# Cross attention on one core: denominators from columns of ones beside the values, a fifth score bank, and an exponential in two parts

## The reference

```python
x = (hidden - mu) * rsqrt(var + eps) * gamma + beta        # hidden: 32 x 56 x 512
Q = split_heads(x @ Wq.T)                                  # 32 heads of 16
K = V = split_heads(ctx)                                   # ctx: 32 x 1500 x 512
scores = einsum('bhsd,bhtd->bhst', Q, K) * 16 ** -0.5      # masked where the mask is false
attn = einsum('bhsd', softmax(scores) @ V)
out = hidden + attn @ Wout.T
```

## Time and profile before

| | |
|---|---|
| median of 3 runs | 1465.87 us (1465.43 to 1465.91) |
| span of the profiled execution | 1461.6 us |
| TensorE busy, matmuls | 1404.7 us (96%), 30000 records |
| VectorE busy | 1079.4 us (74%) |
| ScalarE busy | 750.7 us (51%) |
| GpSimd busy | 1243.8 us (85%) |
| granted TensorE clock, mean | 0.993 |

### The profile page before, as it was taken

How to read it: one execution, slowest core, us unless ns; L and a number is a source line. 1 busy time by engine, 2 the same in 40 slices (tenths; PEclk the granted TensorE clock), 3 DMA queues, 4 the chain that set the end, 5 groups by cost and what they waited for, 6 DMA issues and landing times.

```text
span 1461.6 us, 66063 instructions
## 1 busy us (share of the span) xinstructions
PE 1404.7 (96%) x30000; PEld 992.2 (68%) x30000; DVE 1079.4 (74%) x3356; ACT 750.7 (51%) x623; POOL 1243.8 (85%) x434
## 2 busy tenths in 40 slices
PE   6999999999999999999999999999999999999986
PEld 4346667776777777766776776777777777766765
DVE  6657777777777777777787777777777777777730
ACT  2125555555555555555555555555555555555553
POOL 1009999999999999989999898999999999999996
PEclk8989999999999999999999999999999999999999
DMA  9303444444444344444544434354443444444320
GB/s 297 81 33 148 165 162 160 157 158 168 162 168 172 145 172 157 160 170 147 180 150 166 164 146 175 145 187 160 156 166 142 182 161 161 170 165 156 143 79 21
DMA packets 39161, 224.90 MB, mean 154 GB/s; under 512 B 4546, under 2 KB 4578, under 8 KB 26882
## 3 DMA queue, kind: packets, MB, share of 16 engines
q1 hardware_dynamic: 38882, 220.68, 41.5%
HBM read 216.90 MB, written 3.77 MB: 151 GB/s over the span
## 4 chain that ended last, share of the span: by engine, by line
PE 81%; DVE 10%; ACT 6%; issue 1%; DMA 1%; POOL 1%; ACTq 0%; SPq 0%; DVEq 0%; POOLq 0%
PE ps L237 23%; PE ps L292 19%; PE ps L277 17%; DVE masked L338 9%; PE ps L306 6%; PE ps L269 6%; ACT probs L373 6%; PE ps L254 4%; PE ps L670 4%; PE ps L245 1%; POOL sums L425 1%; DMA v<-in_wq_t 0%; DVE probs L578 0%; DVE den_inv L362 0%; PE ps L661 0%
## 5 line engine op out<-in xcount | busy, mean ns | idle before, releaser
L338 DVE CUSTOM_DVE_ANT_0 masked<-ps,mask_tile 112x500 bf16<-112x500 f32 x1536 | 980.0, 674 | 304.9 <-PE ps L237 286.0
L373 ACT ACTIVATE probs<-ps,mask_bias 125x1792 f32<-125x1792 f32 x384 | 673.9, 1755 | 616.6 <-PE ps L277 609.5
L425 POOL TENSOR_TENSOR sums<-sums,probs 125x1792 f32<-125x1792 f32 x191 | 763.1, 3995 | 14.6 <-ACT probs L373 5.7
L425 POOL TENSOR_TENSOR sums<-probs 125x1792 f32<-125x1792 f32 x96 | 383.7, 3997 | 179.5 <-ACT probs L373 177.9
L237 PE MATMUL ps<-kT,qdb 32*112 32x500 bf16 x1536 | 485.5, 413 | 19.6 <-DVE tile_max L338 15.7
L277 PEld LDWEIGHTS ps<-qd,kT 32*125 32x125 f32 x12288 | 423.7, 184 | 1.9 <-issue 0.9
L277 PE MATMUL ps<-qd,kT 32*125 32x112 f32 x12288 | 421.4, 268 | 0.8 <-issue 0.6
L292 PE MATMUL ps<-probs,v 125*32 125x112 f32 x12288 | 373.1, 261 | 2.1 <-issue 1.3
L292 PEld LDWEIGHTS ps<-probs,v 125*32 125x32 f32 x12288 | 298.8, 110 | 70.0 <-issue 46.2
L237 PEld LDWEIGHTS ps<-kT,qdb 32*112 32x112 bf16 x1536 | 161.3, 123 | 217.2 <-DVE tile_max L338 151.2
L269 PE MATMUL ps<-max_rows,ones_row 4*125 4x448 bf16 x1536 | 179.6, 392 | 14.3 <-ACT probs L373 11.1
(11 more groups left out here) (49 smaller groups left out, 256.2 us busy)
## 6 DMA issues: line engine op xcount, KB each, us to landing
kT<-in_kt SPq DMA_DIRECT2D x96, 1000.0 KB, 5.1
v<-in_ctx SPq DMA_DIRECT2D x96, 1000.0 KB
mask_tile<-mask_add SPq DMA_DIRECT2D x32, 328.1 KB, 13.7
x_res<-in_x SPq DMA_DIRECT2D x16, 224.0 KB, 14.3
out<-result SPq DMA_DIRECT2D x16, 224.0 KB, 13.9
probs<-in_x SPq DMA_DIRECT2D x14, 224.0 KB, 9.2
v<-in_wq_t SPq DMA_DIRECT2D x1, 1024.0 KB, 6.1
woutT<-in_wout_t SPq DMA_DIRECT2D x1, 1024.0 KB, 20.6
```

The costliest lines, as they stand in the source:

```text
L338: nc.vector.tensor_tensor_reduce(out=masked[0:PAIR_Q, t % 2, :], in0=bank[0:PAIR_Q, 0:KEYS], in1=mask_tile[0:PAIR_Q, b % 2, KEYS * c:KEYS ...
L373: nc.scalar.activation(probs[0:LANES, k % PROBS], ps[0:LANES, 0:TILES_R, 0:BANK_Q], ACT.Exp, bias=mask_bias[0:LANES, n:n + 1], scale=SCALE ...
L425: nc.gpsimd.tensor_tensor(total, before, probs[0:LANES, slot % PROBS], ALU.add).then_inc(summed, 1)
```

## The change

- **Values.** A chunk of values is loaded into a staging buffer (`v_stage`, two of them). GpSimd copies it (`spread_values`) into `v`, where each pair of heads now has 48 columns: 16 of one head, 16 of ones, 16 of the other. The ones are set once.
- **times_values.** 32 matmuls instead of 16, each with 56 columns of `probs` (one head's queries) and 32 weight columns: this head's 16 values and the 16 ones. The product has the head's output in one half of the rows and its denominator in the other.
- **Sums.** `add_slot`, `add_denominators` and `last_denominators` are gone. ScalarE copies the whole accumulator once a batch (`take_acc`), GpSimd picks the halves (`fold_heads`: two multiplications of 448 columns, two additions of 224), VectorE swaps halves of the denominators within 32 partitions (`swap_denominators`, behind t1 of slot 3), and inverts them as before.
- **Score banks.** Bank 5 is free of denominators. Row tile 3 of the scores alternates between banks 3 and 5. The exponential is two instructions: banks 0 to 2 (125x1344), then the fourth (125x448). The scores of the next slot wait for the first part alone, and for the second part of the slot before the last.
- **Rows.** The turned maxima go through the ring of banks 6 and 7 as a unit of their own, in slot 10 between t2 and t3; VectorE copies them out and GpSimd spreads them.

```diff
-            wait_over(pe, exped, SLOTS * b + k)
+            n = SLOTS * b + k
+            wait_over(pe, exped_held, n)
+            wait_over(pe, exped, n - 1)
...
         def times_values(pe, b, k):
-                pe.wait_ge(v_landed[c], 16 * (b + 1))
+                pe.wait_ge(v_ready, CHUNKS * b + c + 1)
+            pe.wait_ge(exped, SLOTS * b + k + 1)
             if k == 0:
-                wait_over(pe, heads_taken, b)
-            for g in range(BLOCKS):
+                wait_over(pe, acc_taken, b)
+            for i in range(HEAD_GROUPS):
+                g, e = i // 2, i % 2
                 for r in range(TILES_R):
-                    mm = nc.tensor.matmul(acc[ROW * r:ROW * (r + 1), g, :], v[0:LANES, c, k % CHUNK, col:col + ROW],
-                                          probs[0:LANES, k % PROBS, r, PAIR_Q * g:PAIR_Q * (g + 1)],
+                    mm = nc.tensor.matmul(acc[ROW * r:ROW * (r + 1), i, :],
+                                          v[0:LANES, c, k % CHUNK, TILES_R * g + r, HEAD_DIM * e:HEAD_DIM * e + ROW],
+                                          probs[0:LANES, k % PROBS, r, QUERIES * i:QUERIES * (i + 1)],
...
+            nc.scalar.activation(probs[0:LANES, k % PROBS, 0:HELD_ROWS], ps[0:LANES, 0:HELD_ROWS, 0:BANK_Q], ACT.Exp,
+                                 bias=bias, scale=SCALE).then_inc(exped_held, 1)
+            nc.scalar.activation(probs[0:LANES, k % PROBS, HELD_ROWS], ps[0:LANES, score_bank(n, HELD_ROWS), 0:BANK_Q],
+                                 ACT.Exp, bias=bias, scale=SCALE).then_inc(exped, 1)
...
+        def spread_values(pool, b, c):
+            n = CHUNKS * b + c
+            pool.wait_ge(v_landed[n % STAGES], 16 * (n // STAGES + 1))
+            wait_over(pool, pv_done, CHUNK * (n - CHUNKS + 1))
+            halves = v[0:LANES, c].rearrange("p k i (h d) -> p (k i) h d", d=HEAD_DIM)[:, :, 0:3:2, :]
+            staged = v_stage[0:LANES, n % STAGES].rearrange("p k (i h d) -> p (k i) h d", h=2, d=HEAD_DIM)
+            nc.gpsimd.tensor_copy(halves, staged).then_inc(v_ready, 1)
...
+        def fold_heads(pool, b):
+            pool.wait_ge(acc_taken, b + 1)
+            pick_half(picked_den, 1).then_inc(den_picked, 1)
+            pick_half(picked, 0).then_inc(head_picked, 1)
...
+            nc.gpsimd.tensor_tensor(den_across[:], picked_den[:, :, 0], picked_den[:, :, 1], ALU.add).then_inc(den_added, 1)
...
-                for a in range(ADDS):
-                    if (b, a) != (end, ADDS - 1):
-                        add_slot(pool, b, a)
...
-                    if k >= 6 and (k - 6) % GROUP < 2:
-                        add_denominators(pe, b, (k - 6) // GROUP, (k - 6) % GROUP)
-                    elif k in (2, 3) and b > 0:
-                        add_denominators(pe, b - 1, SUMS - 1, k - 2)
-                    if k == ROWS_SLOT and b < end:
-                        turn_rows(pe, b + 1)
+                    for unit in slot_rows(b, k):
+                        turn_rows(pe, unit)
```

More of the change, by code:

```diff
@@ L28 @@
 PROBS = 4
-GROUP = 4
-SUMS = SLOTS // GROUP
-ADDS = SUMS * (GROUP - 1)
+HEAD_GROUPS = 2 * BLOCKS
+PAIR_COLS = 3 * HEAD_DIM
+STAGES = 2
+RING_BANKS = [6, 7]
+HELD_ROWS = TILES_R - 1
+LAST_ROW_BANKS = [3, 5]
+ACC_BANK = 4
+SWAP_AT = (3, 1)
 INVERT_AT = [(3, 3), (4, 0), (4, 2), (4, 3)]
 ROWS_SLOT = 10
+HALVES_SWAPPED = [(lane + HEAD_DIM) % ROW for lane in range(ROW)]
 OUT_PARTS = 4
@@ L59, in slot_others, with slot_rows, slot_units @@
             if slot == k and after % 2 == b % 2 and b >= after]
+def slot_rows(b, k):
+    return [("rows", b + 1)] if k == ROWS_SLOT and b + 1 < BATCH else []
+def slot_units(b, k):
+    tiles = slot_tiles(b, k)
+    return tiles[0:3] + slot_rows(b, k) + tiles[3:4] + slot_others(b, k)
 FIRST_TILES = [("tile", 0, t) for t in range(MAX_TILES)] + [("tile", 1, t) for t in range(AHEAD)]
-RING = FIRST_TILES[:]
-RING += [unit for b in range(BATCH) for k in range(SLOTS) for unit in slot_tiles(b, k) + slot_others(b, k)]
+RING = FIRST_TILES + [("rows", 0)]
+RING += [unit for b in range(BATCH) for k in range(SLOTS) for unit in slot_units(b, k)]
 LAST_OUTS = [("out", d, part) for d in range(BATCH // 2 - 2, BATCH // 2) for part in range(OUT_PARTS)]
@@ L312, in last_denominators @@
-        def last_denominators(pe):
-            pe.wait_ge(summed, ADDS * BATCH - 1)
-            for source in (sums[0:LANES, (SUMS * BATCH - 1) % 2], probs[0:LANES, (SLOTS - 1) % PROBS]):
-                for e in range(2):
-                    for r in range(TILES_R):
-                        own_q = source[:, r, :].rearrange("p (g e q) -> p g e q", g=BLOCKS, e=2)[:, :, e, :]
-                        mm = nc.tensor.matmul(den[ROW * r:ROW * (r + 1), :, :], ones[0:LANES, e, :], own_q,
-                                              start=False, stop=True, skip_group_check=True,
-                                              tile_position=(0, ROW * r))
-            mm.then_inc(den_done, 1)
@@ L338, in take_tile @@
             nc.vector.tensor_tensor_reduce(
-                out=masked[0:PAIR_Q, t % 2, :], in0=bank[0:PAIR_Q, 0:KEYS],
+                out=sums, in0=bank[0:PAIR_Q, 0:KEYS],
                 in1=mask_tile[0:PAIR_Q, b % 2, KEYS * c:KEYS * (c + 1)], scale=1.0, scalar=LOWEST,
@@ L595, in _ @@
             take_max(dve, 0)
-            for unit in FIRST_TILES[MAX_TILES:]:
+            for unit in FIRST_TILES[MAX_TILES:] + [("rows", 0)]:
                 take_unit(dve, unit)
```

227 lines of the change are left out of this document (114 added, 113 removed).

## The result

The changed kernel takes 1586.73 us in the median of four runs (1581.49 to 1588.83), against 1465.65 (1464.49 to 1465.91) for the kernel before on the same chip: a ratio of 1.0825, 95% interval 1.0805 to 1.0845. It is slower by 121 us, where 1413.0 (1396 to 1445) was forecast.

The account below looks back on a forecast made before the run. It took a loop over VectorE's two tiles and TensorE's values to bound ordinary slots. Terms -47.0 - 1.2 - 5.8 + 1.5 = -52.5 us gave 1409.1 profiled, 1413.4 in all; 1398 to 1430 at chance 0.72, stated range 1396 to 1445.

Parts of the forecast that it names:

- What bounds the kernel: Ordinary slots: a loop over VectorE's two tiles and TensorE's values, 3.44 us with L306, 3.05 without.
- the exponential's loop: Scores, exponential, next scores: 3.23 us a slot, bare in the last batch, elsewhere only delaying scores inside a slot.
- the split: Exponential in two parts: its loop falls from 3.23 to 2.86 us, no gain of its own in ordinary slots.
- Denominators: Taking L306 off TensorE: five slots of a batch gain 0.39 us each, 1.95 us a batch.
- copies: GpSimd's three copies of 2048 elements a batch: 4.6 us each taken, range 2.3 to 4.57, hidden.
- end: After the last slot: denominators through ScalarE's copy, picks, an addition and a shuffle before the inversions, about 1.5 us more.
- the cover over GpSimd: GpSimd's chain to slot 3's denominators: 13.6 us with 16.0 available, hidden until a copy takes 5.8 us.
- the turned maxima stand in the ring: Slot 10: the turned maxima wait until VectorE has taken t1, no gain there and a loss of 0.08 us.
- Values: the step that failed: Values in 64 records for 32, priced by columns: 0.02 us more a slot, 0.25 a batch.
- the floor for narrow matmuls: Case in the list of chances called only the floor: 1425 us, chance 0.08.
- the rival of values by the record: Values limited by issue, not columns: 1.54 us a slot, 1701 us; chance 0.10, wholly or in part and slower.
- Signs given: Profile after: values 0.92 us, t3 to t3 3.07, last batch 2.86 a slot; wrong if the batch stays above 41.

Follow-up runs that it names:

- the 112-column kernel: Changed kernel with 16 values matmuls of 112 columns instead of 32 of 56, one head's output of each pair left out: 1408.42 us, ratio 0.9609.
- the new denominators with one exponential: Changed kernel with 16 values matmuls of 112 columns and the exponential again one instruction over four banks, bank 5 unused: 1446.9 us, ratio 0.9874.
- a quarter: Changed kernel whose loads bring only a quarter of keys (from the third batch) and values (from the second): 1486.49 us, ratio 1.0125.
- next to nothing loaded: Changed kernel whose loads bring only 32 columns of each chunk of keys (from the third batch) and values (from the second): 1440.34 us, ratio 0.9844.
- with 56 columns: Kernel before with its values in 32 matmuls of 56 columns instead of 16 of 112, same result: 1596.45 us, ratio 1.0907.
- half and half: Changed kernel with 24 values matmuls a slot, in each row tile four of 56 columns and two of 112: 1455.02 us.

## Why the prediction was wrong, step by step

*What bounds the kernel.* Right for the changed kernel, half right for the one before. t3, VectorE's two tiles, t2, values is a loop of 3.44 with L306 and 3.05 without; the 112-column kernel runs at 3.06. Its middle batches take 40.57 us in the mean; the forecast of 42.11 - 1.62, without the 0.25 for narrow matmuls, was 40.24. But I wrote of the kernel before that the exponential's loop only delays scores inside a slot. There L269 waits for it 217 times, and slots 1, 2, 5 and 6 take 3.24 from scores to scores, with L306 or without:

```profile
PEld ps L269 <- ACT probs L373: 64.7, 217, 1.3
```

Both loops hold that kernel. So the new denominators with one exponential give little, 18 us, and the split, which I priced at nothing of its own in ordinary slots, 38; their sum of 56 is near the forecast's 52.5 and the 8 that the narrow matmuls were to take.

*Denominators, split, copies, end.* Right, as terms. With 112 columns the whole comes to 1408.42 where the working gave 1405 once the extra matmuls' price was out. ScalarE's parts take 1381 and 626 ns (1.38 and 0.5 to 0.6 said), VectorE's copy and its shuffle 274 and 407 (some 0.2 and 0.3 said, from no row), and GpSimd's copies 1.89 us, less even than the lower end of 2.3; the other end of that range, 4.57, was the one I took, and it was hidden all the same.

```profile
L385 ACT ACTIVATE probs<-ps,mask_bias 125x1344 f32<-125x1344 f32 x384 | 530.3, 1381 | 711.9 <-PE ps L303 711.9
...
L387 ACT ACTIVATE probs<-ps,mask_bias 125x448 f32<-125x448 f32 x384 | 240.4, 626 | 0.0
...
L429 POOL COPY v<-v_stage 125x2048 f32<-125x2048 f32 x96 | 181.5, 1891 | 75.5 <-DMA v_stage<-in_ctx 75.4
```

The last slots, without tiles, run at 1543.34, 1546.18, 1549.02: 2.84 each, for the forecast of 2.86 and the 3.23 of the earlier trace rows.

```profile
1543.34 0.41 PE L295 MATMUL ps<-max_rows,ones_row 4*125 4x448 bf16 x4 [0.65 <-ACT probs L385]
...
1546.18 0.41 PE L295 MATMUL ps<-max_rows,ones_row 4*125 4x448 bf16 x4 [0.65 <-ACT probs L385]
...
1549.02 0.41 PE L295 MATMUL ps<-max_rows,ones_row 4*125 4x448 bf16 x4 [0.65 <-ACT probs L385]
```

VectorE waits for the swapped denominators (`den` on `den_across`) only in two batches of 32, so the cover over GpSimd held. In slot 10 L269 now waits for VectorE 0.83 each time (24.9 us in 30), because the turned maxima stand in the ring. It costs what the earlier trace rows gave, 0.08: from t3 to t3 slot 10 takes 5.08 in the 112-column kernel, for 5.01 before.

*Values: the step that failed.* The working took 0.02 a slot for the narrow matmuls, 0.25 a batch; they cost 5.49 a batch (46.06 for 40.57). As the pace of the matmuls 0.02 is right. 64 records end after 0.99, groups of four start 0.049 apart, as worked out from columns. A price by the record, 1.54 for 64 records, is out with that. No run shows the floor for narrow matmuls that the recorded chances name (1425): the groups of 56 columns start 0.049 apart, half of the 0.096 between groups of 112 in the trace of before. What I did not price is the supply. I wrote "TensorE must now take 104 pairs of load and matmul in a slot for 72" in the rival of values by the record, but looked for a limit only in the values' own 0.77 us ("by the record, 1.54"), not in how long 256 instructions have to last. The row that would have told it was on the page of before and I left it out: 236 packets in 1461.6 us, one every 6.2 us, and 5.4 by the records of an ordinary slot. The forecast needed one every 3.8 us in ordinary slots and every 4.1 in the mean of a batch (40.49 us for 2554 instructions), beside 1 MB loads. This is a rival that should have had a good chance, with a price that no row could give.

*The rival's mechanism.* Its outcome (slower than before) came, with 0.10 given, not its working. It stands at 1701 for values that last 1.7 us; the values last 0.92. What was lost comes in late blocks, 38 of them 1.3 to 3.5 us long and 53 shorter, and as a second effect in the clock: the granted clock falls to 0.5, mostly for 3.4 or 6.8 us, 208.8 us in all (20.5 before).

*Signs given.* "I am wrong if the batch stays above 41 us": it takes 46.06 in the mean. "t3 to t3 of 3.07 in all ordinary slots" holds roughly in those without a stall: from scores to scores, by the medians over the batches, six of the twelve slots take 3.06 to 3.28, but slots 3, 6 and 7 take 5.06, 5.11 and 4.24, where long stalls fall (with 112 columns 4.40, 2.96 and 3.04).

*What stays open.* How the loss splits between late blocks and the lower clock can only be bounded (107 and up to 82 us). That a block's packet starts late where data is under way is in the traces, and the runs with a quarter and with next to nothing loaded fit it; in what order the DMA engines serve the two is not seen. No run spreads the loads and leaves the mask and the residual in time. What holds slot 6 once slot 5 has become shorter wasn't followed up.

## What to carry over

Before a change that raises the number of TensorE's instructions, divide its loads and matmuls by 256, the block of these traces, and ask how long a block lasts: here 5.5 us cost little (14 late blocks, 12.2 us), 4.5 some 3%, and 3.8 cost 13% while 1 MB loads ran. A cost by columns can be right to a hundredth and the kernel still lose, so read the instruction queue's row beside the busy times. Where two loops of a slot are level, as here 3.23 and 3.05 to 3.44, an edit that shortens one alone brings little: it takes both. And an edit that moves some loads of SyncE moves all that stand behind them in its order: here VectorE's wait for the residual rose from 3.2 to 41.2 us.

## What the runs showed of the hardware

- TensorE's instructions came in packets of 16384 bytes. With 256 instructions in each, the waiting ones included, 321 were worked out and 320 are on the page of the changed kernel; 236 and 236 before, 332 and 331 with 56 columns, 225 and 225 with 112, 273 and 273 half and half. In the eight traces of the table packets never started less than 3.25 us apart.
- A late block stopped TensorE in the middle of a group of matmuls, 0.3 to 3.5 us in the changed kernel, and the profile calls it "issue". TensorE went on 1.39 us (median) after the packet had landed.
- In the changed kernel the packet started later where data packets were under way: 2.5 us (median) after the first instruction of the block before with ten or more, where 53 of 70 blocks were late, and 0.9 with fewer than four, where 6 of 114 were.
- Such an idle time was often followed by a granted clock of 0.5: 36 of the 39 falls of the changed kernel after the first 100 us came less than 6 us after the start of a late block, and 28 records took 1.86 us for 1.03.
- Float32 matmuls of 56 columns in four column tiles cost by columns: four records every 0.049 us, for 0.096 with 112 columns.
